# A decoder's attention on one core: separate staging buffers for q and k, a ring of four pairs of heads, and the negated row maxima moved by DMA into a 97th row of the exact scores

## What is computed

```python
a = jax.nn.softmax(jnp.einsum('bhsd,bhtd->bhst', q, k) * scale, axis=-1)
o = jnp.einsum('bhst,bhtd->bhsd', a, v)
```

```python
x = _layernorm(x + _L0_attn_ref(x, ...))      # "splat": 16 dims a head, 256 keys
x = _layernorm(x + _L0_xattn_ref(x, ctx))     # "cross0": 16 dims, 120 keys
x = _layernorm(x + _L0_ffn_ref(x, ...))
x = _layernorm(x + _L1_attn_ref(x, ...))      # "causal": 16 dims, 256 keys
x = _layernorm(x + _L1_xattn_ref(x, ctx, ..)) # "self1" and "cross1": 32 dims, 256 and 120 keys
x = _layernorm(x + _L1_ffn_ref(x, ...))
```

## Time and profile before

| | us |
|---|---|
| median of three executions | 4110.17 |
| lowest, highest | 4107.24, 4129.73 |
| the profiled execution | 4104.28 |
| its span in the trace | 4102.6 |
| PE busy | 3208.5 (78%) |
| DVE busy | 2695.7 (66%) |
| ACT busy | 2103.1 (51%) |
| POOL busy | 975.7 (24%) |

### The profile page before, as it was taken

The page is one execution under the profiler, slowest core; times in us unless marked ns, Lnnn a source line. Parts: engine busy times, 40 slices in busy tenths (PEclk is TensorE's granted clock), DMA queues, the critical chain, the costliest instruction groups (busy, mean ns, idle before and its releaser), DMA issues. The chain is left out here.

```text
span 4102.6 us, 87404 instructions
## 1 busy us (share of the span) xinstructions
PE 3208.5 (78%) x34864; PEld 2496.1 (61%) x34864; DVE 2695.7 (66%) x6135; ACT 2103.1 (51%) x4254; POOL 975.7 (24%) x1793
## 2 busy tenths in 40 slices
PE   2878687888687878877977868797867797878776
PEld 1666465766575657656755657575646675756654
DVE  5767575766575757756766657585756676757665
ACT  4645464555455555544554545545545555446542
POOL 1312341122122321221233122211332122114310
PEclk9989898988898989888988989898988897989987
DMA  6221211112112111121111111212111112112110
GB/s 185 73 59 49 70 53 55 48 51 65 45 53 68 48 58 54 39 65 52 56 57 58 51 51 40 66 52 63 60 50 52 50 44 71 50 54 67 53 36 6
DMA packets 339974, 233.26 MB, mean 57 GB/s; under 512 B 67937, under 2 KB 311538, under 8 KB 339570
## 3 DMA queue, kind: packets, MB, share of 16 engines
q1 hardware_dynamic: 339570, 227.68, 18.8%
HBM read 122.23 MB, written 105.38 MB: 55 GB/s over the span
## 5 line engine op out<-in xcount | busy, mean ns | idle before, releaser
L1164 ACT ACTIVATE p<-bank,p_log 128x512 f32<-128x512 f32 (+2 forms) x1280 | 749.6, 586 | 1118.3 <-PE bank L855 1013.6
L1718 POOL TENSOR_TENSOR prob<-p,prob 120x256 f16<-120x256 f32 (+2 forms) x512 | 452.3, 883 | 1841.4 <-ACT prob L1165 1841.0
L1423 DVE TENSOR_REDUCE negm<-bank 128x2 f16<-128x512 f32 (+1 forms) x1280 | 675.4, 569 | 147.6 <-PE bank L818 140.1
L1165 ACT ACTIVATE prob<-bank,p_log 128x512 f16<-128x512 f32 (+2 forms) x1280 | 751.2, 587 | 0.0
L834 PE MATMUL bank<-q_ring,k_ring 80*128 80x256 f16 (+4 forms) x2048 | 459.2, 292 | 124.6 <-DVE made L1374 90.7
L1353 DVE TENSOR_TENSOR prob<-p,prob 128x512 f16<-128x512 f32 (+2 forms) x768 | 481.3, 636 | 94.0 <-ACT prob L1165 90.3
L725 PE MATMUL bank<-w_exp,ident_h 128*128 128x512 f16 x1280 | 426.3, 418 | 133.9 <-DMA k_ring<-k_heads 121.2
L855 PE MATMUL bank<-ident_h,negm 128*128 128x256 f16 (+2 forms) x2560 | 456.6, 267 | 0.0
L818 PE MATMUL bank<-k_ring,q_ring 80*128 80x256 f16 (+4 forms) x2560 | 373.7, 262 | 75.9 <-DVE negm L1423 62.8
L818 PEld LDWEIGHTS bank<-k_ring,q_ring 80*128 80x128 f16 (+1 forms) x2560 | 239.0, 105 | 283.8 <-DVE negm L1423 72.4
L1727 POOL TENSOR_SCALAR_AFFINE_SELECT probm<-prob 128x128 f16<-128x128 f16 x1024 | 323.8, 354 | 342.5 <-DVE prob L1353 342.5
(11 more groups left out here) (295 smaller groups left out, 6307.0 us busy)
## 6 DMA issues: line engine op xcount, KB each, us to landing
q_ring<-q_heads SPq DMA_DIRECT2D x192, 160.0 KB, 2.6
q_heads<-made SPq DMA_DIRECT2D x192, 128.0 KB
k_heads<-made SPq DMA_DIRECT2D x192, 128.0 KB
q_heads<-made SPq DMA_DIRECT2D x96, 256.0 KB
k_heads<-made SPq DMA_DIRECT2D x96, 256.0 KB
q_ring<-q_heads SPq DMA_DIRECT2D x128, 192.0 KB, 2.7
k_ring<-k_heads SPq DMA_DIRECT2D x128, 160.0 KB, 2.8
k_ring<-k_heads SPq DMA_DIRECT2D x64, 192.0 KB, 3.1
```

What stands on the lines that cost most here:

```text
L1164: act(p32[0:n, g % PBUF32, 0:cols], ps[0:n, 0:cols], ACT.Exp, bias=p_log[0:n, :], scale=a.scale)
L1165: act(prob[0:n, 0, g % PBUF, 0:cols], ps[0:n, 0:cols], ACT.Exp, bias=p_log[0:n, :], scale=a.scale).then_inc(a_done, one(a_done))
L1423: v.tensor_reduce(negm[:, h * NT:(h + 1) * NT], ring_v[bank_of(e, v_full)][:, :].rearrange("p (t n) -> p t n", t=NT)[:, :, 0:ATTNS[k].keys ...
L1718: g.tensor_tensor(prob[0:n, 1, m % PBUF, 0:cols], p32[0:n, m % PBUF32, 0:cols], prob[0:n, 0, m % PBUF, 0:cols], ALU.subtract).then_inc(pp_ ...
```

## The change

Three things are changed together. First, `made` becomes two buffers, `q_made` and `k_made`, so that the highs of k wait for the stores of the k of the phase before, not for those of the q just made. Both head sizes now store three planes (96 rows for 16-dim heads too, a third of them zeros or partly so; the product of the two low parts is left out). Second, the ring holds four pairs of heads in place of three quads; a fill fetches one pair. Third, `exact_scores` loses its L855 matmuls. The contraction gets a 97th row: in `k_ring` it is ones, written once in setup, and in `q_ring` it holds the negated row maxima, one for each query. A DMA for each head (two in the causal attention) moves them there from the column `negm`: 128 partitions of two fp16 values become one row of 256. So that the two values of a partition belong to neighbouring queries, the row scores of the other attentions take every second query as weights (a stride of two elements). PE waits for `max_moved` before the exact scores of a pair. `LATE_SOON` for self1 moves from turns 23, 25, 27 to 22, 24, 25.

```diff
-QUAD, QUADS, SLOTS = 4, 4, 3
-Q_PLANES = (0, 1, 0, 1)
-K_PLANES = {3: (0, 0, 1), 4: (0, 0, 1, 1)}
+SLOTS = 4
+STACKED = 96
+PLANES = {"q": (0, 1, 0), "k": (0, 0, 1)}
...
-LATE_SOON = {1: (("xT", 18), ("q", 21), ("k", 23), ("v", 28)), 3: (("xT", 23), ("q", 25), ("k", 27), ("v", 28))}
+LATE_SOON = {1: (("xT", 18), ("q", 21), ("k", 23), ("v", 28)), 3: (("xT", 22), ("q", 24), ("k", 25), ("v", 28))}
...
 def stored_ahead(k, b, what):
 
-    if what == "k":
-        return STORED[k, b, "q"]
     p = PHASE[k, b]
-    return STORED[(*PHASES[p - 1], "k")] if p > 0 else 0
...
+    return STORED[(*PHASES[p - 1], what)] if p > 0 else 0
...
+def max_moves(a):
+
+    return NT if a.causal else 1
...
-        made = pair("made", 4, TOK)
-        q_ring, k_ring = (sb(f"{what}_ring", [96, SLOTS, QUAD, TOK], F16) for what in "qk")
...
+        made = {what: pair(f"{what}_made", 4, TOK) for what in "qk"}
+        q_ring, k_ring = (sb(f"{what}_ring", [STACKED + 1, SLOTS, PAIR, TOK], F16) for what in "qk")
...
+                step(g.memset(k_ring[STACKED:STACKED + 1, :, :, :], 1.0))
...
-                            last = mm(ps[:, i * TOK:i * TOK + n], q[:, i * P:i * P + P], kk[:, 0:n],
+                            rows = q[:, i * P:i * P + P] if a.causal else q.rearrange("r (p i) -> r i p", i=NT)[:, i, :]
+                            last = mm(ps[:, i * TOK:i * TOK + n], rows, kk[:, 0:n],
                                       start=i == 0, stop=i == NT - 1 and not a.causal)
...
                         ps = slot("a", "p", g)
+                        if g == pair[0]:
+                            e.wait_ge(max_moved[g // PAIR % SLOTS], maxima_in(g // PAIR))
                         for j, (k0, n) in enumerate(a.key_tiles):
                             i0 = j * P if a.causal else 0
-                            mm(ps[0:n, j * TOK:j * TOK + TOK - i0], kk[:, k0:k0 + n], q[:, i0:TOK],
-                               start=j == 0, stop=False)
-                        e.wait_ge(*moved("max", g))
...
-                            last = mm(o, negm[:, h * NT + i:h * NT + i + 1].broadcast_to([P, n]), moving,
-                                      start=False, stop=i == NT - 1)
...
+                def move_maxima(m):
+                    for g in (m * PAIR, m * PAIR + 1):
+                        a, h = ATTNS[ORDER[g][0]], ORDER[g][2]
+                        e.wait_ge(*moved("max", g))
+                        for i in range(max_moves(a)):
+                            n = NT // max_moves(a)
+                            e.dma_start(q_ring[STACKED:STACKED + 1, m % SLOTS, g % PAIR, i * P:i * P + n * P].rearrange(
+                                            "o (p n) -> o p n", n=n),
+                                        negm[:, h * NT + i:h * NT + i + n], allow_slow_non_contiguous=True
+                                        ).then_inc(max_moved[m % SLOTS], 16)
...
-                        begin = max((2 * quad - 4) * TURNS + 2, PLACE[(k, b), "k"] + 0.5)
-                        sends.append((begin + 0.1, quad, "fill"))
+                    for m in range(p * HEADS // PAIR, (p + 1) * HEADS // PAIR):
+                        begin = max((m - SLOTS + 1) * TURNS + 2, PLACE[(k, b), "k"] + 0.5)
+                        sends.append((begin + 0.1, m, "fill"))
+                        sends.append((m * TURNS + 0.3, m, "maxima"))
```

More of the change, by code:

```diff
@@ L407, in decoder @@
         stored = semaphore("stored")
+        max_moved = [semaphore(f"max_moved{slot}") for slot in range(SLOTS)]
         ring_full = [semaphore(f"ring_full{slot}") for slot in range(SLOTS)]
@@ L844, in exact_scores @@
-                        for i in range(NT):
-                            if a.causal:
-                                o = ps[0:n, 0:P] if i == 0 else ps[0:n, P:TOK + P].rearrange("p (j c) -> p j c", j=NT)
-                                times = 1 + i
-                            else:
-                                o, times = rows[:, 0:len(a.key_tiles), i * P:i * P + P], len(a.key_tiles)
-                            moving = ident_h[:, :]
-                            if a.causal and i == 0:
-                                pass
-                            else:
-                                moving = moving.rearrange("p (a n) -> p a n", a=1).broadcast_to([P, times, P])
-                            last = mm(o, negm[:, h * NT + i:h * NT + i + 1].broadcast_to([P, n]), moving,
-                                      start=False, stop=i == NT - 1)
+                            last = mm(ps[0:n, j * TOK:j * TOK + TOK - i0], kk[:, k0:k0 + n], q[:, i0:TOK],
+                                      start=j == 0, stop=not a.causal and k0 + n == a.keys)
@@ L1387, in split_heads @@
                     n = a.keys if what == "k" else TOK
+                    high, low = (made[what][:, part, 0:a.tiles, 0:n] for part in range(2))
                     if not a.splat and not a.causal:
                         for m in range(0, a.tiles, 2):
-                            lows(made[:, 1, m:m + 2, 0:n], made[:, 0, m:m + 2, 0:n],
+                            lows(low[:, m:m + 2, :], high[:, m:m + 2, :],
                                  lambda ps: ps[:, :].rearrange("p (t n) -> p t n", t=2)[:, :, 0:n], 1 / W_SCALE)
                         return
-                    at = next_half(what, k, b)
-                    tiles = raw[:, at:at + a.tiles, 0:n]
+                    r = next_half(what, k, b)
+                    tiles = raw[:, r:r + a.tiles, 0:n]
                     if a.causal:
-                        last = low_part(made[:, 1, 0:a.tiles, 0:n], tiles, made[:, 0, 0:a.tiles, 0:n])
+                        last = low_part(low, tiles, high)
                     else:
@@ L1823, in store @@
                         e.dma_start(to[:, plane * a.dim:(plane + 1) * a.dim].rearrange("c d t n -> c d (t n)"),
-                                    made[:, part, 0:a.tiles, :].rearrange("p t n -> p (t n)")).then_inc(stored, 16)
-                def fill(quad):
-                    k, b = PHASES[quad // QUADS]
-                    a, n = ATTNS[k], quad % QUADS
-                    if n == 0:
+                                    made[what][:, part, 0:a.tiles, :].rearrange("p t n -> p (t n)")).then_inc(stored, 16)
```

85 lines of the change are left out of this document (42 added, 43 removed).

## The result

The changed kernel takes 4655.6 us (median of four, 4650.6 to 4663.9), the kernel before beside it 4110.1 (4107.2 to 4129.7). The ratio is 1.132 (95% interval 1.128 to 1.136). The forecast of 4086 us and its whole range are missed; the sign is that of rival (b), the size is beyond it.

The account below looks back on a forecast made before the run. The prediction took both PE's work and PE's waits on `made` to bound the kernel. L855 removal, the move, the buffers and the clock summed as 4104.3 - 124 + 109 - 23 + 20 = 4086 us, range 3830 to 4240.

Parts of the forecast that it names:

- rival (b): Maxima-to-exponentials loop: a slow landing of the moves becomes the bound, 4199 us at 2.6, 4280 at 3.0; chance 0.22.
- 30 + 70 + 136: Staging waits: 30 us from late self1 phases, 70 from other waits, 136 in the 26 phases of 32-dim heads.
- -124: Exact scores: removing the L855 matmuls saves 0.375 us a step, counted in 377 steps at 0.88, 124 us.
- 109 + 87 + 126: Waits for moves: 109 us for the move itself, 87 behind k's store, 126 behind q's store.
- a little more: Causal heads: their moves of the maxima take slightly over the 2.0 us assumed for the others; no size given.
- +20: Granted clock: a term that adds 20 us to the forecast time.
- -23: Two staging buffers: net gain of 23 us, summed as -10 + 87 - 30 - 70; ends -320 and +60.
- replaced by an equal one: In 26 phases of 32-dim heads, PE's wait for `made` becomes one for moves behind q's store, 0.4 us shorter.
- Most of that is not lost: Between maxima and exact scores: 274 of 640 pairs lack 325 us of room, mostly absorbed by PE's lag and float.
- 172 light steps: Steps shorter than 3.4 us, where the next part's loop sets the time: each costs 0.28 us more, 48 us.
- (a): At the stores: moves slip past and the staging waits vanish, 3769 us, or 3930 for half of it; chance 0.32.
- (c): Row scores' weight loads: a stride of two slows them, adding 51 us, to 4137 us; chance 0.10.

## Why the forecast was wrong

The steps between the two kernels, each the difference of two medians along one path from before to after, beside the terms of the forecast that belong to them:

| step | measured | forecast |
|---|---|---|
| three planes, ring of pairs, turns | -41 | 0 |
| separate staging buffers | -246 | -236 (30 + 70 + 136) |
| the maxima's matmuls removed | +17 | -124 |
| moves, landing needed a step later | +44 | 0 |
| landing needed in the step (4-byte moves) | +429 | +322 (109 + 87 + 126) |
| 2-byte elements in the causal attention | +343 | "a little more" |
| the clock | in the rows above | +20 |
| sum | +546 | -18, or -24 from the median |

The forecast's sum for the buffers, -23, mixes two rows. It let 136 us of the old waits be "replaced by an equal one", 10 us shorter, and so booked neither the gain nor the 126 us of new waits. Taken apart it gives 236 us to the buffers and 126 + 87 = 213 us to moves caught behind stores.

**The causal moves** are the largest error, 343 us: "for causal heads it is a little more" was one phrase for a different form, 128 elements of 2 bytes, for which no row of the trace had a likeness. The range took the other moves up to 3.8 us. A causal pair's maxima take 8.9 us (median) from the last of them to the last landing; this form needed a term and an end of its own.

**The removal of L855** was priced by the durations of its matmuls and counted in 377 steps, because PE is busy 88% of the time outside its waits. That step failed, by 141 us. A busy engine isn't by that the one whose work sets the time: 1280 matmuls more, or 2560 fewer, moved the time by 5 and 17 us. The granted clock followed PE's work (0.921, 0.915, 0.884 in the runs refilled, with the matmuls, and without), and the rest of the saving became idle time. Which wait ends last in those steps was not traced.

**The move.** Its duration was right: 2.0 us in the median for 128 elements of 4 bytes, 0.3 above the row of 1.7. The room for it was wrong. The step that failed is "Most of that is not lost, since PE lags one step and a step that has waited gives float to the next". The trace of before had 274 of 640 pairs with less than 2.0 us between the maxima and the exact scores, lacking 325 us; the forecast charged 0.28 us to each of 172 light steps and half of the lack to 102 other pairs, 109 us. With 4-byte moves PE waits 290 times and 600 us, of which by the count 262 are the 2 us themselves. So most of the lack came as waits. What they cost in time apart from the waits behind stores, no run isolates; together they cost 429 us where the forecast had 322.

**Moves behind stores.** The capture is real and was sized well: 213 us in the forecast, 240 us of PE's waits by the count in the kernel with 4-byte moves, of which stores by head leave 41. Late issues, 98 us of waits there, had no term.

**The staging buffers** were sized well too, 236 and 246 us. The gain was not all idle time: when the waits went, PE's busy time fell by 84 us as well, at a clock of 0.915 in place of 0.887.

**SP.** "The waits of SP are in the order in which DVE and PE finish: nothing" was wrong at the first fill of a late phase, which waits for a DMA's landing, not for an engine. Before, only other fills and stores were queued behind it; now moves are, 12 pairs by 11 us in the changed kernel.

**The clock.** No run shows the forecast's +20 us as a term by itself. What the runs show is the clock beside PE's waits for moves: 0.799 with 320 of them, 2.8 us on average, where the kernel before has 0.884; 0.837 with 4-byte moves, 600.5 us of waits; 0.883 there with filler ahead of the exact scores, 494.4 us. A stream matmul takes 458 ns on average in the changed kernel, before 418. In the kernel before, the granted clock is 1.00 in each of the microseconds from 464 to 470, in which PE idles 4.01 us, and 0.50 in those from 471 to 473; over 470 to 480 it is the 0.83 of the earlier trace rows.

**Rivals.** (b) named the right mechanism, short waits for the moves in the light steps, but had it decide from 2.1 us on; the waits came at 2.0, and with those behind stores they cost 429 us. Of (a) the premise fell, since moves behind a store landed after 6 and 9 us, though the gain that it saw, 290 us from the staging waits, is nearly what the kernel without moves has, 287 with the 41 of the other parts. (c) didn't happen: the weight loads of the row scores take 114 ns on average, not over 150, and of the runs without moves 108 with the stride and 105 without it. The bound that the forecast set on its own mechanism, 700 us of waits for moves, was passed at 891; with 4-byte moves, at 600, it would have held.

## What to carry over

Before a short matmul is replaced by a DMA, count the slack between the producer's end and the consumer's start for every step: expect each step with less room than the landing, here 2.0 us, to pay, and so each that stands behind a store or a waiting DMA in the same queue. Price every form of the DMA by itself, above all one with another element size (here 5.6 us with elements of 2 bytes, 1.8 with 4). Take matmuls away only where PE's work sets the time; try first what filler put in or left out does to it (here 1280 matmuls put in moved 3840 us by 5). When a change has several parts, run them apart: here two gained 287 us and the third lost 832.

## What the runs showed of the hardware

- Four DMAs within SBUF of 0.2 KB, issued one after the other, land in 1.8 us each (median) as 64 elements of 4 bytes, and in 5.6 as 128 elements of 2 bytes, the first after 3.0 and the last after 7.3. Two DMAs of 128 elements of 4 bytes land in 2.0.
- A 4-byte move issued right behind a store of four heads lands after 6.1 to 9.6 us; behind the same store cut into DMAs of 32 rows, after 2.0 in the median, and no move of that kernel takes over 3.8.
- 1280 matmuls of 512 columns added to this kernel cost no time (3835 us against 3840), with the granted clock at 0.921 instead of 0.884.
